# Causal attention ahead of a routed expert layer: when a turn's products are issued among the scores, and the order of the pieces

## What is computed

```python
q = _lora(x, Wq, Aq, Bq).reshape(B, T, H, dh).transpose(0, 2, 1, 3)
k = _lora(x, Wk, Ak, Bk).reshape(B, T, H, dh).transpose(0, 2, 1, 3)
v = _lora(x, Wv, Av, Bv).reshape(B, T, H, dh).transpose(0, 2, 1, 3)
s = jnp.einsum('bhqd,bhkd->bhqk', q, k) / jnp.sqrt(jnp.float32(dh))
s = s + slopes[:, None, None] * (i - j)
s = jnp.where(j <= i, s, NEG_INF)
out = jnp.einsum('bhqk,bhkd->bhqd', jax.nn.softmax(s, axis=-1), v)
x = _layernorm(x + out @ Wp.T)
x = _layernorm(x + experts(x))     # top 2 of 8, capacity 1076 rows each, gelu
```

## Time and profile before

| | us |
|---|---|
| median of three runs | 1210.37 |
| lowest and highest | 1207.93, 1211.15 |
| the profiled execution: time | 1213.11 |
| the profiled execution: span of the core | 1211.0 |
| TensorE busy (its ends are modelled) | 1145.4 (95%) |
| ScalarE busy | 873.1 (72%) |
| VectorE busy | 629.7 (52%) |
| GpSimd busy | 299.0 (25%) |

### The profile page before, as it was taken

How to read it: one execution, slowest core, us unless ns; L and a number is a source line. 1 busy time by engine, 2 the same in 40 slices (tenths; PEclk the granted TensorE clock), 3 DMA queues, 4 the chain that set the end, 5 groups by cost and what they waited for, 6 DMA issues and landing times. The chain is left out here.

```text
span 1211.0 us, 23951 instructions
## 1 busy us (share of the span) xinstructions
PE 1145.4 (95%) x8592; PEld 496.6 (41%) x8592; DVE 629.7 (52%) x1832; ACT 873.1 (72%) x1109; POOL 299.0 (25%) x377
## 2 busy tenths in 40 slices
PE   9999999999999999999999998879999999999980
PEld 4332222222222222222222211157777777777760
DVE  5644333232355526634362400467777777777757
ACT  2889999999999999999999998624334334334314
POOL 5421211111112221330322221021333333333340
PEclk9999999999999999999999998979999999999995
DMA  5733331422321332131412110164535643553216
GB/s 177 182 111 77 98 83 42 101 68 77 94 75 63 90 75 68 37 103 36 109 31 83 30 35 10 30 213 83 122 85 73 132 106 39 122 118 40 26 20 277
DMA packets 119301, 104.20 MB, mean 86 GB/s; under 512 B 59223, under 2 KB 104508, under 8 KB 119184
## 3 DMA queue, kind: packets, MB, share of 16 engines
q1 hardware_dynamic: 101720, 76.90, 24.4%
q0 software_dynamic: 15968, 24.12, 9.1%
q10 hardware_dynamic: 1496, 1.68, 0.4%
HBM read 48.07 MB, written 47.96 MB: 79 GB/s over the span
## 5 line engine op out<-in xcount | busy, mean ns | idle before, releaser
L1497 ACT ACTIVATE prob<-ps_s 128x1024 f32<-128x1024 f32 (+4 forms) x841 | 709.3, 1009 | 42.1 <-PE ps_s L1380 40.0
L1397 PE MATMUL ps_o<-prob,v_aug 128*17 128x512 f32 (+3 forms) x3236 | 421.1, 569 | 3.0 <-DVE acc L1581 2.3
L1380 PE MATMUL ps_s<-qop,kop 51*128 51x512 f16 (+3 forms) x1618 | 273.2, 370 | 14.6 <-issue 4.1
L2462 ACT ACTIVATE hid<-ps_h,b 128x384 f32<-128x384 f32 (+1 forms) x192 | 107.2, 559 | 229.2 <-PE ps_h L2405 223.6
L1380 PEld LDWEIGHTS ps_s<-qop,kop 51*128 51x128 f16 x1618 | 66.0, 93 | 399.4 <-ACT prob L1497 360.1
L2421 PE MATMUL ps_y<-w2s,hs 128*128 128x256 bf16 (+1 forms) x1728 | 189.8, 273 | 0.1
L2405 PE MATMUL ps_h<-xs,w1s 128*128 128x384 bf16 (+1 forms) x1152 | 186.4, 315 | 0.0
L1581 DVE COPY acc<-ps_o 32x512 f32<-32x512 f32 (+2 forms) x108 | 74.2, 688 | 206.5 <-PE ps_o L1397 204.8
L2379 POOL DMA_INDIRECT result<-y,entry x72 | 116.5, 1619 | 248.9 <-DVE y L2493 219.9
L2421 PEld LDWEIGHTS ps_y<-w2s,hs 128*128 128x128 bf16 (+1 forms) x1728 | 159.8, 99 | 25.5 <-issue 3.1
L1533 POOL TENSOR_SCALAR_AFFINE_SELECT prob<-prob 128x256 f32<-128x256 f32 (+1 forms) x179 | 68.3, 393 | 311.5 <-ACT prob L1497 309.8
(11 more groups left out here) (201 smaller groups left out, 688.8 us busy)
## 6 DMA issues: line engine op xcount, KB each, us to landing
w<-in_W SPq DMA_DIRECT2D x16, 1024.0 KB, 8.0
slots_x<-empty POOLq DMA_DIRECT2D x12, 520.0 KB, 4.1
qop<-fparts_q SPq DMA_DIRECT2D x42, 128.0 KB, 4.8
aT<-attnT SPq DMA_DIRECT2D x16, 256.0 KB
x_all<-in_x SPq DMA_DIRECT2D x8, 512.0 KB
result<-x_all SPq DMA_DIRECT2D x8, 512.0 KB, 3.5
x_all<-result SPq DMA_DIRECT2D x8, 512.0 KB, 6.5
out<-x_all SPq DMA_DIRECT2D x8, 512.0 KB, 2.6
```

Of the source, the lines that this page charges most:

```text
L1380: mm = pe.matmul(ps_s[:, u.p % SLOTS_S, e, a.q0:], o.key(e, a.h, a.kt), o.query(e, a.h, a.b, a.q0), start=True, stop=True)
L1397: mm = pe.matmul(ps_o[32 * c:32 * c + VW, a.q0:], o.v[:, a.kt, a.h], prob[:, t % RING, c % 2, c // 2, a.q0:], start=a.first, stop=a.last)
L1497: act.activation(prob[:, t % RING, n, e:z, q0:], ps_s[:, u.p % SLOTS_S, e:z, q0:], ACT.Exp, scale=1.0 / (SCALE * SCALE)).then_inc(exp_done, 1)
L2462: act.activation(hid[:, q % HB, 0:w], ps_h[:, q % HB, 0:w], ACT.Gelu_apprx_tanh, bias=b1[:, e, q % HC:q % HC + 1]).then_inc(gelu, 1)
```

## The change

Products no longer stand a fixed two turns behind. `LATER` has a digit for each turn: how many units of scores are issued behind the turn's last unit before its products. 66 turns have 2, 84 have 3, 152 have 4, 55 have 5, 50 have 6, and the last two 1 and 0; whatever would come behind the last unit is issued there turn by turn. `PRODUCTS_AT` lists the turns whose products come behind a given unit, so several may follow one another. A piece stands behind the first unit of its turn or, if its turn is in `BEHIND` (74 of 123), behind the second. The pieces' tables are given anew, 59 of the 123 turns differ, mostly by one. VectorE takes pieces and copies in the same new order as TensorE; all that hung on `LAG` now hangs on `PRODUCTS_TURN`. A wait for the values of a new tile of keys is added ahead of the first products that read them.

```diff
-LAG = 2
+LATER = [int(c) for c in
+            ('6664664226425344534642334246422334264245645445534246424444444246424435345364534453453444444642424344'
...
+BY_UNIT = [(t, n) for t in range(N_STEPS) for n in range(2) if STEPS[t][n]]
+PRODUCTS_AT, PRODUCTS_TURN = {}, []
+for _t in range(N_STEPS):
+    _p = max(u.p for u in STEPS[_t] if u) + LATER[_t]
+    _at = BY_UNIT[_p] if _p < len(UNITS) - 1 else (max(N_STEPS, PRODUCTS_TURN[-1] + 1), 0)
+    PRODUCTS_AT.setdefault(_at, []).append(_t)
+    PRODUCTS_TURN.append(_at[0])
-STORE_AT = {t: [j for j in JOBS if j.end + LAG == t] for t in range(N_TURNS)}
+STORE_AT = {t: [j for j in JOBS if PRODUCTS_TURN[j.end] == t] for t in range(N_TURNS)}
...
+BEHIND = (0, 4, 6, 9, 13, 15, 17, 23, 27, 29, 31, 39, 41, 45, 47, 51, 55, ...)
+PIECE_BEHIND = {t: int(t in BEHIND) for t in PIECES}
...
                 def pv(t):
                     units = [(n, u) for n, u in enumerate(STEPS[t]) if u]
+                    if t in NEW_KEYS:
+                        pe.wait_ge(j.v_out, 2 * (NEW_KEYS[t] + 1))
...
                             if u:
                                 score(u)
-                            if n == 0:
+                            if n == PIECE_BEHIND.get(t):
                                 piece_of(t)
+                            for done in PRODUCTS_AT.get((t, n), ()):
+                                pv(done)
                     else:
-                        piece_of(t)
-                    if t >= LAG:
-                        pv(t - LAG)
+                        for done in PRODUCTS_AT[t, 0]:
+                            pv(done)
...
-                    if t in PIECE_AT:
-                        kind, *of = PIECE_AT[t]
...
-                    for job in STORE_AT[t]:
-                        evict(job)
+                    for n in range(2):
+                        if n == PIECE_BEHIND.get(t):
+                            kind, *of = PIECE_AT[t]
...
+                        for done in PRODUCTS_AT.get((t, n), ()):
+                            for job in ENDED[done]:
+                                evict(job)
                     if t in SPLIT_X_AT:
                         j.dve_split_x(dve, *SPLIT_X_AT[t])
```

More of the change, by code:

```diff
@@ L319, with stores_until @@
 assert FLAG_TURN < BLOCK_END[NB - 1]
-EARLY_TURN = max(j.end + LAG for j in JOBS if any(b == NB - 1 and h >= H // 2 for _, b, h in j.heads)) + 1
+EARLY_TURN = max(PRODUCTS_TURN[j.end] for j in JOBS if any(b == NB - 1 and h >= H // 2 for _, b, h in j.heads)) + 1
 EARLY_SCALE_AT = {EARLY_TURN + 4 + _s: _s for _s in range(KT)}
 assert FLAG_TURN < EARLY_TURN and max(EARLY_SCALE_AT) < N_TURNS
-assert all(j.end + LAG > FLAG_TURN for j in JOBS for _, b, h in j.heads if b == NB - 1 and h < H // 2)
-def stores_until(end):
-    return [max([j.stores for j in JOBS if j.number % ACCS == k and j.end <= end], default=0) for k in range(ACCS)]
+assert all(PRODUCTS_TURN[j.end] > FLAG_TURN for j in JOBS for _, b, h in j.heads if b == NB - 1 and h < H // 2)
+def stores_until(turn):
+    return [max([j.stores for j in JOBS if j.number % ACCS == k and PRODUCTS_TURN[j.end] < turn], default=0) for k in range(ACCS)]
 PIECES = sorted(PIECE_AT)
@@ L339 @@
 BEFORE = {z: PIECE_AT[a] for a, z in zip(PIECES, PIECES[1:])}
+PIECE_BEHIND = {t: int(t in BEHIND) for t in PIECES}
+assert set(BEHIND) <= set(PIECES) and PIECES[-1] < N_STEPS
+NEW_KEYS = {min(t for t in range(N_STEPS) for u in STEPS[t] if u for a in u.tiles.values() if a.kt == _kt): _kt for _kt in range(T // P)}
 CLEAR_X_AT = {8 + 11 * (4 * k + i): (k, a, z) for k in range(4) for i, (a, z) in enumerate(((0, 4), (4, 8), (8, 12), (12, ROWS_X)))}
@@ L1441, in _ @@
                 block_of = 0
-                for t in range(N_STEPS + LAG):
+                for t in range(N_TURNS):
                     if t == 0:
@@ L2159, in vector @@
         dve.wait_ge(r.last_loaded, 48)
-        for k, stored in enumerate(stores_until(N_STEPS)):
+        for k, stored in enumerate(stores_until(N_TURNS)):
             dve.wait_ge(l.out_stored[k], stored)
```

74 lines of the change are left out of this document (34 added, 40 removed), and 5 rows, old and new, of the table HALF_AT.

## The result

The changed kernel took 1194.28 us (median; 1193.35 to 1196.06), the kernel before 1210.2 in the same comparison. The ratio is 0.9864, with an interval of [0.9838, 0.9889]: 16 us faster, inside the range and 7 us short of the 1187.4 forecast. The profiled execution took 1195.21 us, its span is 1193.2, against 1211.0: 17.8 us. That is some 2 us more than between the medians, since the profiled execution of before (1213.11) was 2.7 us slower than its median of 1210.37 and that of after 0.9.

What follows compares the result with a forecast made beforehand. TensorE was taken to bound where pieces are dense, ScalarE elsewhere. Fewer changes 15, copies 5, diagonals 2 and open transition 1 made 23 us: 1211.0 to 1188 on the span, 1187.4 on the median; range 1176 to 1203.

Steps and rivals of the forecast that it cites:

- What bounds the kernel: Attention: TensorE bounds where pieces are dense, ScalarE elsewhere, each stopping the other; ScalarE's idle before exps 42 to about 25 us.
- 24 us less work on TensorE: Attention loop: fewer changes between scores, products and pieces, at 0.10 and 0.12 us each, take 24 us off TensorE.
- 13 to 17 of it count: Attention stretches of about 20 turns: 13 to 17 of 24 us shorten the time; the rest falls where ScalarE bounds.
- Diagonals, 2 us: After a diagonal's short tiles ScalarE runs out, some fourteen stops; short products behind the next full scores gain 2 us more.
- Copies, 5 us: Waits for VectorE's copy of a finished head, 9.1 us in 18 places: the new order gains 5 us.
- The stop at turn 206: VectorE's copy starts late behind the router's choices, ScalarE stops 1.52 us; copy ahead of the choices gains 1.5 us.
- the 0.8 at the end of the loop: Wait of 0.95 us for a finished head's copy at 773.16 us: 0.8 us of it counted as gained.
- The waits that the change adds, nothing: Products two units behind (66 turns) wait for their own exp, but the next score needs it too: no cost.
- The rest as long as before: Part behind attention, bound by its own loads behind the last products: same length, starting earlier by the whole gain.
- Rival 1: Double products in attention starve ScalarE; slower if 70 places lose over 0.34 us each, 1228 us at 0.6; chance 0.09.
- Rival 3: Attention: the stretches gain but the stops are only moved; 8 to 12 us gained, 1200 us; chance 0.13.
- Rival 5: TensorE, with less to do, idles longer and gets the low clock more often; no separate chance given.

Runs made afterwards that it cites:

- unpair: Changed kernel with 51 double products taken apart, the second turn's products one unit later, where copies of finished heads keep their room: 1198.9 us, ratio 0.9892.
- loop4: Changed kernel with products of turns 361 to 378 put back to four units of scores behind, instead of two or three: 1195.42 us in one run.
- pairs_all: Kernel before, with its old pieces, but the products of every two turns together behind the same unit: 1268.16 us, ratio 1.0464.
- loop_pairs: Changed kernel with turns 361 to 376 in pairs of products and turns 377 and 378 four units behind: 1196.79 us in one run.
- products_only: Changed kernel's new places of the products, with the piece tables of the kernel before, each piece behind its turn's first unit: 1218.71 us, ratio 1.0062.
- split_late: Changed kernel with GpSimd's casts three turns later in five of seven blocks, and behind their turn's exps in all: 1192.49 us, ratio 0.9848.

## Why the prediction was right, and where not

- **What bounds the kernel: right.** ScalarE's waits fell by 13 us and its span by 19; TensorE-bound stretches gained most (turns 160 to 199: 4.1).
- **24 us less work on TensorE: right**, 26.7 by the ledger, 23 to 25 with common short distances. For the open transition, a piece with products behind it, I took the upper end of 0 to 0.12, and it is that end. Timeline of after, a half piece with products behind, and two turns of products:

```profile
78.97 0.83 PE L682 MATMUL ps_r<-xs_half,ws_half 128*128 128x256 f16 x6
79.73 1.05 PE L1401 MATMUL ps_o<-prob,v_aug 128*17 128x512 f32 x8
80.71 0.82 PE L1382 MATMUL ps_s<-qop,kop 51*128 51x512 f16 x6
...
87.06 1.91 PE L1401 MATMUL ps_o<-prob,v_aug 128*17 128x512 f32 x16
88.91 0.45 PE L1382 MATMUL ps_s<-qop,kop 51*128 51x256 f16 x6
```

  Half to products is 79.73-78.97 = 0.76, as half to score in the earlier trace rows. Two turns are 88.91-87.06 = 1.85, against 2x0.98 apart; less the 0.98 of a turn ahead of a score, the first is 0.87, where the last products had given 0.86. The other 2.7 us of the 26.7 are within the ledger's own error: its short distances are uncertain by some 0.01 us, at about 1,300 transitions.
- **13 to 17 of it count: right in size, at its lower end**, by unpair (0.4 to 0.6 of each us, which is 10 to 14 of 24). Turns 180 to 199 in about 38: 38.26.
- **Diagonals, 2 us: right in kind.** Behind short turns of products, without the turns at the branch, ScalarE was idle for 10.2 us in 21 places before and 7.0 in 14 after, 3.4 of these where three stand in a row, 1.44 of them at turn 229.
- **Copies, 5 us: this step failed.** The waits for copies were 9.1 us in the earlier trace rows and are

```profile
PEld ps_o L1401 <- DVE acc L1586: 8.8, 14, 1.5
```

  in after, and 14.6 and 15.1 by the ledger. The stop at turn 206 went, but stops of 1.13 to 1.24 came at turns 238, 325 and 359, and with GpSimd's casts moved 0.4 is left of each of the first two and nothing of the third. I read the late copy as VectorE's order and didn't ask why a subtraction of 128x32 took 1.01 us. The new order left the casts in their turns and put other copies behind them. Turn 206 came free as forecast, 2.0 us in turns 200 to 219, but VectorE's order was only half of its cause: the old order gives the same with the casts moved. Of the 0.8 at the end of the loop about 0.2 came: the waits inside the products of turn 402 went from 1.05 to 0.84 us.
- **The waits that the change adds, nothing: mis-sized.** Products and pieces wait 13.3 instead of 1.5. Most is moved from the scores (loop4), but turn 229 lost 1.2, on GpSimd's scatter, which I had not counted among the queues that the products are moved past, and turns 361 to 378 lost 0.7 (the rest of the 1.1 there is a cast's). I had "the masked one is last in its group" as protection; it was the one that waited.
- **The rest as long as before: the part is, its start isn't.** I set the start of the rest by the last exp; it is set by the last products, 1.2 later against the exps than before. I had written myself that its loads start behind the last products.
- **Sum.** Forecast 23 on the span; measured 17.8. Missing: copies 5, turn 229 and the loop 2, the last products 1.2, 8.2 in all; against it up to 2.7 more of work, of which by the share above some 1.5 counts. That makes 16.3, and 1.5 us are left, no more than the start of attention moves between runs. By the medians the gain is 16 and not 17.8, so nothing is left to explain there.
- **Rival 1** was the mechanism of pairs_all and not of the change: 0.24 a double, under the 0.34. **Rival 3**, half, was nearer to the measured time than the forecast's middle, and in kind it is what happened to the copies: the stops were moved. **Rival 5** didn't come in the change: the granted clock is 1.00 from 29 to 708 us. It came twice in pairs_all, for 3.4 us each. The Trainium skill warns of short idles between groups of matmuls (TensorE: Matmul & The Clock Gate, A second HAM failure mode); the trace of after, with 60 double products, doesn't show it, and that of pairs_all does, behind idles of about 0.5 us.

Open: why the clock fell at those two places of pairs_all and not at the others; why a double costs 0.11 in loop_pairs, 0.24 in after and 0.47 in pairs_all, beyond that TensorE is the later the more pieces stand near; and why each half of the change alone loses so much before scores (products_only) was read from the ledger, and not tested further.

## What to carry to other kernels

Count the changes of kind on TensorE and price them from starts of neighbouring rows, but take only the share that falls where TensorE is the longer engine. An order is fitted as a whole: here each of two halves was slower alone, though one of them had nearly all of the saved work. And when a small VectorE step takes five times its usual time, look at what GpSimd does in that moment before you blame the order: the order can be at fault too, and moving the GpSimd instruction alone tells the two apart.

## What the runs showed of the hardware

In these traces a VectorE `tensor_tensor` on two SBUF operands that meets a GpSimd cast or subtraction already under way ends only when GpSimd's has ended: a subtraction of 128x32 takes 1.01 us instead of 0.19, a square of 128x256 1.43 instead of 0.28, a subtraction of 128x4 1.57 instead of 0.17, and each ends within 0.02 to 0.15 us behind GpSimd's. So it was with all 11 that started beside such a GpSimd operation in the loop of before and all 12 of after; in split_late one of three (a comparison of 128x64 at 336.3) took 0.16 us all the same. Casts from PSUM beside them keep their 0.42. GpSimd's masks do it too, for less: a square of 128x256 in before took 0.79 us beside two masks at 63.8 us. The Trainium skill, SBUF — State Buffer, Who interferes with whom, says the same: VectorE and GpSimd share one pair of ports as an exclusive lock, held for the whole instruction, and a `tensor_tensor` with both inputs in SBUF contends with GpSimd's reads. The trace agrees: the seven subtractions had a mean of 896 ns, which is six at 1.01 us and one at 0.19, and with the casts moved all seven took 0.19.
